# Stack loads split in two halves by heads, the maxima's transfer issued from the scalar engine's queue

## The chip, the cores and the metric

The kernel runs on one core of one Trainium2 chip. The metric is the device time of one execution in microseconds (us), as the median of several runs; lower is better.

## What is computed

For 32 sequences of 256 positions with 128 channels, `x` is normalised to `xn` (layer norm), and the result is `x + attention(xn) + ffn(xn)`:

```python
# attention: 16 heads of 8 channels, causal, rotated q and k, a decay bias per head
scores = einsum('bhqd,bhkd->bhqk', q_rot, k_rot) / sqrt(8) + decay_bias      # 16 heads x 256 x 256
attn = softmax(where(causal, scores, -inf))
out = einsum('bhqk,bhkd->bhqd', attn, v) @ Wo.T
# ffn: routing weights rw over 8 experts, one causal attention with mixed q, k, v, then
# a mixture of 8 experts with gelu, weighted by rw2
q = einsum('btc,ech,bte->bth', n1, q_proj, rw)       # k, v alike; output through o_proj with rw
hs = xn + attn_out
return hs + moe_out
```

## The kernel before

The work of the 32 sequences is a pipeline of 32 steps, `step(n, u, n_x)`, written out by hand once for each engine; each engine has its own program and its own order, and they meet through semaphores. Step n finishes the attentions of sequence n, finds the row maxima of sequence n+1, and computes projections, rotation and routing weights of sequence n+2. After the 32 steps comes the expert part (16 blocks), which the change doesn't touch.

**The stacks.** The scores are computed by matmuls over 128 rows that stand stacked in `qst` and `kst` (bfloat16, 128 partitions x 2 buffers x 16 heads x 256 positions; buffer `u` or `par` is n mod 2). Rows 8 to 55 and the like hold q and k, each split in three bfloat16 parts; other rows hold the decay bias; rows `R_MAX` to `R_MAX + 2` of `qst` hold the negated row maxima, also in three parts. The vector engine leaves the rotated parts in `parts`; SP stores them to DRAM (`store_parts`, semaphore `parts_stored`) and `stacks(b, par, old)` reads them back in stack form: one transfer of zeros to the rows of the maxima, then six into `qst` (8 rows each) and three into `kst` (24, 16 and 8 rows). Ten transfers, all counted by `stack_in`.

**First pass, `unit1`.** Twelve units per sequence (units 0 to 5 read heads 0 to 7, units 6 to 11 heads 8 to 15) compute scores with the maxima's rows at zero; the vector engine takes their row maxima (`row_max`), splits them in parts (`max_parts`), TensorE transposes them (`max_T`), ScalarE copies them to `mT` (`evac_max`), and SP sends `mT` to the maxima's rows of `qst` (`put_max`, semaphore `max_in`).

**Second pass, `unit2`.** Twelve units again, in the same order of heads, now with the maxima subtracted; ScalarE takes the exponential (`exps`). `unit2(n, u, 0)` is the one that waits for `max_in`. In step n the second pass of sequence n stands beside the first pass of sequence n+1.

TensorE's order around a step's start is: ..., `max_T(n+1)`, `att_T(n)`, `oe(n, 0)`, `oe(n, 1)`, `att_out(n)`, `oe(n, 2)` to `oe(n, 7)`, then in the next step `norm_T` (four transposes), `unit2(n+1, ..., 0)`, `qk`, `unit2(..., 1)`, `proj`.

SP's order in a step: store the result of the step before (after `base_done`), load two tiles of `x`, spread the routing weights over all partitions (1 MB, `rep`), `store_parts`, `stacks`, `store_weights`, `put_max`. Stacks of sequence n+2 take the buffer of sequence n, so `stacks` waits until all twelve units of its second pass are done:

```python
sp_.wait_ge(s2_out, UNITS * (b - 1))        # b = n + 2
```

ScalarE ends its step with `evac_max(n+1)` and `evac_att(n)` and begins the next with `evac_norm` (`xnT`, `n1T`, `sqT`).

Lines that the prediction speaks of: L1267 `norm_T`, L1330 and L1337 the first pass's score matmuls, L1360 and L1365 the second pass's, L1308 `weights_T`, L385 the zeros, L391 the stack rows, L396 `store_weights`, L407 `put_max`, L621 `evac_max`, L665 `evac_att`, L589 `evac_norm`, L629 the exponential.

Of the kernel before, what the change touches and what calls it, by code (L numbers as in the profile page):

```python
# [15 lines left out]
S = 256  # L16
D = 128
H = 16
DH = D // H
# [5 lines left out]
UNITS = 3 * NG  # L25
# [15 lines left out]
R_PARTS = 8  # L41
R_MAX = R_PARTS + 6 * DH
Q_SLOTS = ((0, 1, 0), (1, 1, 0), (2, 1, 0), (3, 1, 1), (4, 1, 1), (5, 1, 2))
K_SLOTS = ((0, 3, 0), (3, 2, 0), (5, 1, 0))
KR = P
STACK_DMAS = 1 + len(Q_SLOTS) + len(K_SLOTS)

LN2_LINKS = 3 + 10
# [68 lines left out]
def build(nc, x, w_attn, w_o, log_xi, pi_logit, e_logit, ln1_w, ln1_b, ln2_w, ln2_b, sim1, gates1,  # L117
          q_proj, k_proj, v_proj, o_proj, sim2, gates2, w1, w2, c_ident, c_mask_qk, c_mask_kq, c_pos_freq,
          c_sin_sign, c_pos, c_rank, out):
    scr_parts = nc.dram_tensor("scr_parts", (2, 2, 3, DH, H, S), BF16, kind="Internal").ap()  # L120
# [5 lines left out]
    with ExitStack() as ctx:  # L126
# [3 lines left out]
        def sem(name):  # L130
            return ctx.enter_context(nc.semaphore(name))
# [30 lines left out]
        zeros_b = sb("zeros_b", [3, 1, S], BF16)  # L162
# [98 lines left out]
        rot_chain = sem("rot_chain")  # L261
        parts_out = sem("parts_out")
        parts_stored = sem("parts_stored")
        stack_in = sem("stack_in")
        v_out = sem("v_out")
        v_done = sem("v_done")
        s1_out = sem("s1_out")
# [76 lines left out]
        def _(sp_):  # L344
# [31 lines left out]
                    sp_.dma_start(scr_parts[par, side].rearrange("p d h t -> (d h) p t"),  # L376
                                  parts[:, :, side]).then_inc(parts_stored, 16)

            def stacks(b, par, old):

                if old:

                    sp_.wait_ge(s2_out, UNITS * (b - 1))

                sp_.dma_start(qst[R_MAX:R_MAX + 3, par], zeros_b[:].broadcast_to((3, H, S))).then_inc(stack_in, 16)  # L385
                sp_.wait_ge(parts_stored, 32 * (b + 1))
                for side, dst, slots in ((0, qst, Q_SLOTS), (1, kst, K_SLOTS)):
                    v = scr_parts[par, side].rearrange("p d h t -> (p d) (h t)")
                    for first, n, part in slots:
                        rows = dst[R_PARTS + DH * first:R_PARTS + DH * (first + n), par].rearrange("p h t -> p (h t)")  # L390
                        sp_.dma_start(rows, v[DH * part:DH * (part + n)]).then_inc(stack_in, 16)  # L391

            def store_weights(b, par):

# [3 lines left out]
            def spread_weights(b, par):  # L398
# [2 lines left out]
                sp_.dma_start(rep[:, par].rearrange("p e t -> p (e t)"),  # L401
                              scr_rw[par].rearrange("(o e) t -> o (e t)", o=1).broadcast_to((P, E * S))
                              ).then_inc(rep_in, 16)

            def put_max(b, par):
                sp_.wait_ge(mT_done, b + 1)
                sp_.dma_start(qst[R_MAX:R_MAX + 3, par], mT[:]).then_inc(max_in, 16)  # L407

            def load_x(b, par, dst, arrived):
                src = x_v[b] if isinstance(b, int) else x_v[bass.ds(b, 1)].rearrange("o p i c -> p (o i) c")  # L410
# [6 lines left out]
            def step(n, u, n_x):  # L417


                sp_.wait_ge(base_done, n)  # L420
                if not isinstance(n, int) or n > 0:
                    store_base(n - 1, 1 - u)
                load_x(n, u, xr, xr_in)
                if n_x == 3:

                    sp_.wait_ge(x_in, 16 * (n + 3))
                    load_x(n + 3, 1 - u, xt, x_in)
                if n_x:
                    spread_weights(n + 1, 1 - u)
                if n_x >= 2:  # L430
                    store_parts(n + 2, u)
                if n_x >= 2:
                    stacks(n + 2, u, True)
                    store_weights(n + 2, u)
                if n_x:
                    put_max(n + 1, 1 - u)

            store_parts(0, 0)
            stacks(0, 0, False)
            store_weights(0, 0)  # L440
            spread_weights(0, 0)

# [1 line left out]
            sp_.wait_ge(x_in, 32)  # L444
            load_x(2, 0, xt, x_in)
            store_parts(1, 1)
            stacks(1, 1, False)
            store_weights(1, 1)
            put_max(0, 0)
            step(0, 0, 3)  # L450
            step(1, 1, 3)
            with sp_.Fori(1, NB // 2 - 2) as j:
# [112 lines left out]
        def _(act):  # L565
# [52 lines left out]
            def evac_max(b):  # L618
                act.wait_ge(mT_out, b + 1)
                act.wait_ge(max_in, 16 * b)  # L620
                act.activation(mT[:], ps[0:3 * H, S1[0], 0:S // 2].bitcast(BF16), ACT.Copy).then_inc(mT_done, 1)  # L621

            def exps(n, k, last):

                G, i = divmod(k, 3)
                act.wait_ge(s2_out, UNITS * n + k + 1)
                if i == 0:
                    act.wait_ge(pv_out, NG * n + max(G - 1, 0))
                act.activation(pr[:, G % 2, i], ps[:, S2[k % 2]], ACT.Exp).then_inc(exp_done, 1)  # L629

                if last and k >= UNITS - 2:
                    return
                act.wait_ge(exp_done, UNITS * n + k + 1)
                act.activation(ps[:, S2[k % 2]], seeds[:, 1 if (k + 2) % 3 == 2 else 0], ACT.Copy  # L634
                               ).then_inc(seed_done, 1)
# [27 lines left out]
            def evac_att(n):  # L663
                act.wait_ge(attT_out, n + 1)
                act.activation(attT[:], ps[:, PVB, 0:S], ACT.Copy).then_inc(attT_done, 1)  # L665
# [54 lines left out]
            def step(n, u, n_x):  # L720
                if n_x >= 2:
                    evac_norm(n + 2, u)
                for k in range(3):
                    exps(n, k, n_x == 0)
                if n_x >= 2:
                    evac_logits(n + 2)
                if n_x == 0:
                    evac_norm2(0)
                    square2(0)
                for k in range(3, 8):  # L730
                    exps(n, k, n_x == 0)
                    if n_x == 0 and k == 4:
                        evac_norm2(1)
                        square2(1)
                    if n_x == 0 and k == 5:
                        scale_norm2(2)
                    if k == 6:
                        evac_pv(n, 0)
                    if n_x == 0 and k == 6:
                        evac_logits2(0)  # L740
                    if n_x == 0 and k == 7:
                        scale_norm2(3)
                evac_qk(n)
                exps(n, 8, n_x == 0)
                if n_x >= 2:
                    gate_tanh(n + 2)
                if n_x == 0:
                    evac_norm2(2)
                    square2(2)
                exps(n, 9, n_x == 0)  # L750
                if n_x == 0:
                    gate_tanh2(0)
                soft_exp(n)
                exps(n, 10, n_x == 0)
                exps(n, 11, n_x == 0)
                evac_soft(n)
                if n_x == 0:
                    evac_norm2(3)
                    square2(3)
                evac_pv(n, 1)  # L760
                evac_ve(n)
                if n_x >= 2:
                    evac_weights(n + 2)
                    evac_v(n + 2, u)
                if n_x:
                    evac_max(n + 1)
                evac_att(n)
                if n_x == 1:
                    scale_norm2(0)
                    scale_norm2(1)  # L770
                if n_x == 0:
                    evac_weights2(0)
                    evac_logits2(1)

            for b in range(2):
# [3 lines left out]
                gate_tanh(b)  # L779
                evac_weights(b)  # L780
            evac_max(0)
            step(0, 0, 3)
            step(1, 1, 3)
            with act.Fori(1, NB // 2 - 2) as j:
# [465 lines left out]
        def _(pe):  # L1250
# [60 lines left out]
            def unit1(b, par, k):  # L1311
# [4 lines left out]
                    pe.wait_ge(rwT_done, b + 1 if not isinstance(b, int) or b else 2)  # L1316
                if k == 0:

                    pe.wait_ge(stack_in, 16 * STACK_DMAS * (b + 1 if not isinstance(b, int) or b else 2))
                if k == 0:  # L1320

                    pe.wait_ge(mT_done, b)
# [409 lines left out]
```

## Time and profile before

| what | value |
| --- | --- |
| median of 3 runs | 1439.15 us (1437.37 to 1440.41) |
| time of the profiled execution | 1432.54 us |
| its span | 1430.7 us |
| mean granted TensorE clock | 0.984 of full |
| busy: TensorE matmul, VectorE, ScalarE, GpSimd | 90%, 71%, 53%, 15% |
| DMA, mean | 93 GB/s |

The span is the time from the first to the last instruction of the one execution that the profiler recorded; 1.8 us of its time lie around it. Starts in the rows below are us from the span's start. PE is TensorE, PEld its weight loads, DVE VectorE, ACT ScalarE, POOL GpSimd, SP the engine that only issues transfers; SPq and ACTq are the queues of instructions of SP and ACT, and a transfer's row there shows its issue alone, not its landing. The 32 steps lie between 89 and about 1180 us of the span.

### The profile page before, as it was taken

To read this page: it belongs to the slowest core of one execution; us is meant where nothing else is said; L and a number is where in the kernel's file an instruction comes from. 1 tells how busy PE (TensorE), PEld (TensorE's weight loads), DVE (VectorE), ACT (ScalarE), POOL (GpSimd) and SP (SyncE) were. 2 spreads that over 40 slices of the span, in tenths; PEclk is the share of its full clock that TensorE was granted. 3 is DMA by queue.
4 is the path that set the end of the run, shared out by engine and by line. 5 is a ranking of instruction groups with operands and counts; after the bars stand their busy time and mean duration, and the time that the engine had idled before them with its cause. 6 is when DMAs were issued, how large, how long until landed. Compare 5 with 4: busy or idle time off the path is not lost.

```text
span 1430.7 us, 33751 instructions
## 1 busy us (share of the span) xinstructions
PE 1284.3 (90%) x10686; PEld 1016.5 (71%) x10780; DVE 1021.5 (71%) x3882; ACT 762.4 (53%) x1664; POOL 221.6 (15%) x326
## 2 busy tenths in 40 slices
PE   0369999999999999999999999999999979999999
PEld 0247777777778777777777777777777767777776
DVE  8557777777777777777777777777776656677754
ACT  1125655665555555555555555555555574455532
POOL 4011112111122211111111111112111200000000
PEclk9679999999999999999999999999999999999999
DMA  4423233223333333333222233223223204554344
GB/s 117 94 54 85 76 77 76 75 76 80 79 85 79 78 76 79 83 90 90 77 75 76 75 83 80 76 75 76 75 76 77 58 9 172 204 202 153 149 153 159
DMA packets 89904, 133.33 MB, mean 93 GB/s; under 512 B 9675, under 2 KB 78395, under 8 KB 78523
## 3 DMA queue, kind: packets, MB, share of 16 engines
q1 hardware_dynamic: 89298, 132.10, 32.6%
q14 instruction: 86, 0.70, 0.2%
q8 instruction: 32, 0.52, 0.2%
q10 hardware_dynamic: 488, 0.01, 0.0%
HBM read 108.76 MB, written 21.50 MB: 91 GB/s over the span
## 4 chain that ended last, share of the span: by engine, by line
PE 63%; DVE 15%; DMA 11%; issue 6%; ACT 4%; DVEq 1%; SPq 0%; ACTq 0%
DMA qst<-mT 10%; PE ps L1663 8%; PE ps L1649 8%; PE ps L1401 7%; PE ps L1402 6%; PE ps L1411 6%; PE ps L1275 4%; PE ps L1379 4%; DVE mx L1025 3%; PE ps L1337 3%; PE ps L1360 3%; PE ps L1333 2%; PE ps L1330 2%; PE ps L1436 1%; PE ps L1383 1%
## 5 line engine op out<-in xcount | busy, mean ns | idle before, releaser
L629 ACT ACTIVATE pr<-ps 128x512 f32<-128x512 f32 x384 | 227.7, 593 | 205.4 <-PE ps L1360 166.7
L1025 DVE TENSOR_REDUCE mx<-ps 128x2 f32<-128x512 f32 (+1 forms) x384 | 263.9, 688 | 46.6 <-PE ps L1330 26.2
L634 ACT ACTIVATE ps<-trn 128x512 f32<-128x512 bf16 x382 | 229.8, 601 | 12.1
L530 POOL TENSOR_TENSOR n1s<-rep,n1T 128x256 f32<-128x256 f32 x256 | 177.0, 730 | 277.4 <-DVE mpart L1037 252.9
L1663 PEld LDWEIGHTS ps<-w2s,ats 128*128 128x128 f32 x1024 | 131.7, 192 | 50.4 <-issue 46.5
L1401 PE MATMUL ps<-n1s,wq 128*128 128x256 f32 x512 | 160.6, 396 | 0.0
L1402 PE MATMUL ps<-n1s,wk 128*128 128x256 f32 x512 | 152.8, 380 | 0.0
L1411 PE MATMUL ps<-wv,n1s 128*128 128x128 f32 x1024 | 150.6, 280 | 0.0
L803 ACT ACTIVATE n1s<-ps 128x512 f32<-128x512 f32 x128 | 76.5, 597 | 123.3 <-PE ps L1649 122.1
L1411 PEld LDWEIGHTS ps<-wv,n1s 128*128 128x128 f32 x1024 | 131.9, 192 | 9.0 <-issue 6.3
L1663 PE MATMUL ps<-w2s,ats 128*128 128x128 f32 x1024 | 135.7, 276 | 1.1 <-DVE ats L1207 1.1
L1649 PE MATMUL ps<-rep,w1s 128*128 128x512 f32 x256 | 130.8, 594 | 0.0
L1446 PE MATMUL ps<-wop,ats 128*128 128x128 f32 x1024 | 125.9, 277 | 0.3 <-DVE ats L1074 0.3
L1360 PE MATMUL ps<-qst,kst 128*128 128x256 bf16 x512 | 98.9, 275 | 29.1 <-DMA qst<-mT 29.0
L1446 PEld LDWEIGHTS ps<-wop,ats 128*128 128x128 f32 x1024 | 120.2, 193 | 0.8 <-DVE ats L1074 0.5
L537 POOL TENSOR_TENSOR zt<-xn,rstd 128x256 f32<-128x256 f32 x32 | 19.6, 612 | 646.9 <-DVE rstd L862 646.9
L1402 PEld LDWEIGHTS ps<-n1s,wk 128*128 128x128 f32 x512 | 97.7, 191 | 13.2
L1337 PE MATMUL ps<-kst,qst 128*128 128x256 bf16 x512 | 98.8, 275 | 0.0
L1401 PEld LDWEIGHTS ps<-n1s,wq 128*128 128x128 f32 x512 | 80.0, 192 | 12.3 <-issue 8.6
L1074 DVE TENSOR_TENSOR ats<-rep,ps 128x512 f32<-128x512 f32 (+1 forms) x160 | 81.4, 575 | 10.2 <-PE ps L1437 9.7
L942 DVE TENSOR_TENSOR rott<-ps,cs 128x512 f32<-128x512 f32 x32 | 22.1, 692 | 92.5 <-PE ps L1275 90.0
L589 ACT ACTIVATE xnT<-ps 128x256 f32<-128x256 f32 x32 | 12.3, 383 | 133.4 <-PE ps L1267 128.4
(225 smaller groups left out, 2281.6 us busy)
## 6 DMA issues: line engine op xcount, KB each, us to landing
rep<-scr_rw SPq DMA_DIRECT2D x32, 1024.0 KB, 5.0
qst<-scr_rw SPq DMA_DIRECT2D x16, 1024.0 KB, 6.5
kst<-scr_rw SPq DMA_DIRECT2D x16, 1024.0 KB, 8.3
scr_parts<-parts SPq DMA_DIRECT2D x64, 192.0 KB, 2.3
qst<-scr_parts SPq DMA_DIRECT2D x192, 64.0 KB
kst<-scr_parts SPq DMA_DIRECT2D x32, 192.0 KB
xt<-in_x SPq DMA_DIRECT2D x32, 128.0 KB, 2.3
kst<-scr_parts SPq DMA_DIRECT2D x32, 128.0 KB
```

Of the source, the lines that this page charges most:

```text
L530: pool.tensor_tensor(n1s[:, e], rep[:, par, e], n1T[:, par], ALU.mult).then_inc(n1s_done, 1)
L629: act.activation(pr[:, G % 2, i], ps[:, S2[k % 2]], ACT.Exp).then_inc(exp_done, 1)
L634: act.activation(ps[:, S2[k % 2]], seeds[:, 1 if (k + 2) % 3 == 2 else 0], ACT.Copy).then_inc(seed_done, 1)
L1025: dve.tensor_reduce(mx[:, min(i, 1), h:h + n], ps[:, S1[k % 2]].rearrange("p (h t) -> p h t", h=n), AX_X, ALU.max, negate=True).then_inc(s ...
L1337: ins = mm(bank[:, h * S:(h + 1) * S], qst[0:KR, par, hh, P:S], kst[0:KR, par, hh, :], start=False, stop=True, skip_group_check=True)
L1360: ins = mm(bank[:, h * S:(h + 1) * S], kst[0:KR, u, hh, 0:P], qst[0:KR, u, hh, :], start=False, stop=True, skip_group_check=True)
L1401: mm(ps[:, QKB, 0:S], wq[:, e], n1s[:, e], start=(e == 0), stop=(e == E - 1), skip_group_check=True)
L1402: ins = mm(ps[:, QKB, S:2 * S], wk[:, e], n1s[:, e], start=False, stop=(e == E - 1), skip_group_check=True)
L1411: ins = mm(ps[:, QKB, i * D:(i + 1) * D], n1s[:, e, i * P:(i + 1) * P], wv[:, e], start=(e == 0 and i == 0), stop=(e == E - 1), skip_group ...
L1446: ins = mm(ps[:, G1, i * D:(i + 1) * D], ats[:, e, i * P:(i + 1) * P], wop[:, e], start=(e == 0 and i == 0), stop=(e == E - 1), skip_group ...
L1649: mm(ps[:, UP[k % 4]], w1s[:, e], n2T[t % 8], start=True, stop=True).then_inc(up_out, 1)
L1663: ins = mm(ps[:, MOE[t % 2], i * D:(i + 1) * D], hgs[:, k % 2, i * P:(i + 1) * P], w2s[:, e], start=(e == 0 and i == 0), stop=(e == E - 1) ...
```

## The change

`stacks` gets a fourth argument, the half. Each half loads the rows of eight heads, with its own zeros and its own semaphore of a pair. The first half waits only for the first six units of the second pass that reads its buffer, the second half for all twelve. Per sequence SP issues 20 transfers of half the size in place of 10. `unit1` waits for the first half ahead of unit 0 and for the second ahead of unit 6. `put_max` goes from SP's program to ScalarE's, where it stands behind `evac_att`.

```diff
+HALF_HEADS = H // 2
...
-        stack_in = sem("stack_in")
+        stack_in = [sem("stack_lo_in"), sem("stack_hi_in")]
...
-            def stacks(b, par, old):
-
+            def stacks(b, par, old, half):
+
+                hh = slice(HALF_HEADS * half, HALF_HEADS * (half + 1))
                 if old:
 
-                    sp_.wait_ge(s2_out, UNITS * (b - 1))
-
-                sp_.dma_start(qst[R_MAX:R_MAX + 3, par], zeros_b[:].broadcast_to((3, H, S))).then_inc(stack_in, 16)
+                    sp_.wait_ge(s2_out, UNITS * (b - 2) + UNITS // 2 * (half + 1))
+
+                sp_.dma_start(qst[R_MAX:R_MAX + 3, par, hh], zeros_b[:].broadcast_to((3, HALF_HEADS, S))
+                              ).then_inc(stack_in[half], 16)
                 sp_.wait_ge(parts_stored, 32 * (b + 1))
                 for side, dst, slots in ((0, qst, Q_SLOTS), (1, kst, K_SLOTS)):
-                    v = scr_parts[par, side].rearrange("p d h t -> (p d) (h t)")
+                    v = scr_parts[par, side].rearrange("p d h t -> (p d) h t")
                     for first, n, part in slots:
-                        rows = dst[R_PARTS + DH * first:R_PARTS + DH * (first + n), par].rearrange("p h t -> p (h t)")
-                        sp_.dma_start(rows, v[DH * part:DH * (part + n)]).then_inc(stack_in, 16)
+                        rows = dst[R_PARTS + DH * first:R_PARTS + DH * (first + n), par, hh]
+                        sp_.dma_start(rows, v[DH * part:DH * (part + n), hh]).then_inc(stack_in[half], 16)
...
-            def put_max(b, par):
-                sp_.wait_ge(mT_done, b + 1)
-                sp_.dma_start(qst[R_MAX:R_MAX + 3, par], mT[:]).then_inc(max_in, 16)
...
                 if n_x >= 2:
-                    stacks(n + 2, u, True)
+                    stacks(n + 2, u, True, 0)
+                    stacks(n + 2, u, True, 1)
                     store_weights(n + 2, u)
-                if n_x:
-                    put_max(n + 1, 1 - u)
...
+            def put_max(b, par):
+                act.wait_ge(mT_done, b + 1)
+                act.dma_start(qst[R_MAX:R_MAX + 3, par], mT[:]).then_inc(max_in, 16)
...
                 evac_att(n)
+                if n_x:
+                    put_max(n + 1, 1 - u)
...
                 if k == 0:
 
-                    pe.wait_ge(stack_in, 16 * STACK_DMAS * (b + 1 if not isinstance(b, int) or b else 2))
+                    pe.wait_ge(stack_in[0], 16 * STACK_DMAS * (b + 1 if not isinstance(b, int) or b else 2))
+                if k == UNITS // 2:
+
+                    pe.wait_ge(stack_in[1], 16 * STACK_DMAS * (b + 1 if not isinstance(b, int) or b else 2))
```

SP's program in a steady step, before (in square brackets the semaphores it waits for):

```order
L376 DMA scr_parts<-parts 128x3x256 [waits parts_out]
L376 DMA scr_parts<-parts 128x3x256
L385 DMA qst<-zeros_b 3x16x256 [waits s2_out]
L391 DMA qst<-scr_parts 8x4096 [waits parts_stored]
L391 DMA qst<-scr_parts 8x4096 x5
L391 DMA kst<-scr_parts 24x4096
L391 DMA kst<-scr_parts 16x4096
L391 DMA kst<-scr_parts 8x4096
L396 DMA scr_rw<-rwT 16x128 [waits rwT_done]
L407 DMA qst<-mT 3x16x256 [waits mT_done]
L415 DMA scr_base<-bs 128x256 [waits base_done]
```

The same place in the changed kernel, from the first half's zeros on:

```order
L387 DMA qst<-zeros_b 3x8x256 [waits s2_out]
L394 DMA qst<-scr_parts 8x2048 [waits parts_stored]
L394 DMA qst<-scr_parts 8x2048 x5
L394 DMA kst<-scr_parts 24x2048
L394 DMA kst<-scr_parts 16x2048
L394 DMA kst<-scr_parts 8x2048
L387 DMA qst<-zeros_b 3x8x256 [waits s2_out]
L394 DMA qst<-scr_parts 8x2048 [waits parts_stored]
...
L399 DMA scr_rw<-rwT 16x128 [waits rwT_done]
L414 DMA scr_base<-bs 128x256 [waits base_done]
```

The ten transfers have become two groups of ten with half as many columns, each group behind its own wait for the second pass, and the maxima's transfer is gone from SP.

ScalarE's program at the end of a step, before:

```order
L616 ACTIVATE rwT<-ps 16x128 [waits rw_stored,rwT_out]
L602 ACTIVATE vst<-ps 128x4x4x8 [waits v_out]
L602 ACTIVATE vst<-ps 128x4x4x8
L621 ACTIVATE mT<-ps 48x256 [waits max_in,mT_out]
L665 ACTIVATE attT<-ps 128x256 [waits attT_out]
```

and in the changed kernel:

```order
L615 ACTIVATE rwT<-ps 16x128 [waits rw_stored,rwT_out]
L601 ACTIVATE vst<-ps 128x4x4x8 [waits v_out]
L601 ACTIVATE vst<-ps 128x4x4x8
L620 ACTIVATE mT<-ps 48x256 [waits max_in,mT_out]
L668 ACTIVATE attT<-ps 128x256 [waits attT_out]
L624 DMA qst<-mT 3x16x256 [waits mT_done]
```

The maxima's transfer now stands on ScalarE, one instruction behind the copy that it waits for. TensorE's order of matmuls is the same in both.

## Rows read from the trace of the kernel before

**Rows 1.** The page: busy time of TensorE; shares of the chain by line

```profile
PE 1284.3 (90%) x10686; PEld 1016.5 (71%) x10780; DVE 1021.5 (71%) x3882; ACT 762.4 (53%) x1664; POOL 221.6 (15%) x326
...
DMA qst<-mT 10%; PE ps L1663 8%; PE ps L1649 8%; PE ps L1401 7%; PE ps L1402 6%; PE ps L1411 6%; PE ps L1275 4%; PE ps L1379 4%; DVE mx L1025 3%; PE ps L1337 3%; PE ps L1360 3%; PE ps L1333 2%; PE ps L1330 2%; PE ps L1436 1%; PE ps L1383 1%
```

**Rows 2.** Who waited for whom: us in total, times, longest us

```profile
PE ps L1360 <- DMA qst<-mT: 29.0, 29, 3.0
...
PEld ps L1360 <- DMA qst<-mT: 7.9, 5, 3.2
```

**Rows 3.** Timeline, TensorE, one step's sixth unit, the next's start: start, us, [idle before]

```profile
615.59 0.39 PE L1365 MATMUL ps<-qst,kst 128*128 128x128 bf16 x4
...
638.10 0.38 PE L1267 MATMUL ps<-ident,zt 128*128 128x128 f32 x2
639.54 0.39 PE L1360 MATMUL ps<-qst,kst 128*128 128x256 bf16 x2 [1.06 <-DMA qst<-mT]
```

**Rows 4.** Timeline, SP's queue, one step: start, us of the issue

```profile
616.77 0.91 SPq L376 DMA_DIRECT2D scr_parts<-parts  x2
627.69 0.78 SPq L385 DMA_DIRECT2D qst<-zeros_b  x1
628.59 2.25 SPq L391 DMA_DIRECT2D qst<-scr_parts  x6
630.88 1.04 SPq L391 DMA_DIRECT2D kst<-scr_parts  x3
...
634.36 0.76 SPq L407 DMA_DIRECT2D qst<-mT  x1
```

**Rows 5.** Stretches of that step: us, PE, PEld, DVE, ACT, POOL, PEclk, DMA share, GB/s

```profile
628.00:633.00 5.00, 4.65 (x48) 3.85 (x47) 4.36 (x23) 2.48 (x6) 0.67 (x1) 1.00 0.52 95
633.00:638.00 5.00, 5.00 (x48) 4.97 (x47) 2.88 (x6) 1.23 (x5) 4.87 (x8) 1.00 0.50 72
```

**Rows 6.** Timeline, TensorE: starts of second passes in steps 1, 10, 11, 29, 30

```profile
127.99 0.39 PE L1360 MATMUL ps<-qst,kst 128*128 128x256 bf16 x2 [0.55 <-DMA qst<-mT]
...
433.29 0.38 PE L1267 MATMUL ps<-ident,zt 128*128 128x128 f32 x2
433.51 0.38 PE L1360 MATMUL ps<-qst,kst 128*128 128x256 bf16 x2
...
466.35 0.38 PE L1267 MATMUL ps<-ident,zt 128*128 128x128 f32 x2
...
1083.95 0.39 PE L1360 MATMUL ps<-qst,kst 128*128 128x256 bf16 x2 [1.13 <-DMA qst<-mT]
...
1117.24 0.39 PE L1360 MATMUL ps<-qst,kst 128*128 128x256 bf16 x2 [0.98 <-DMA qst<-mT]
```

**Rows 7.** Timeline, ScalarE, the same step's end and the next one's start

```profile
633.96 0.37 ACT L621 ACTIVATE mT<-ps 48x256 bf16<-48x256 bf16 x1
634.23 0.37 ACT L665 ACTIVATE attT<-ps 128x256 f32<-128x256 f32 x1
638.60 0.38 ACT L589 ACTIVATE xnT<-ps 128x256 f32<-128x256 f32 x1 [4.00 <-PE ps L1267]
...
640.05 0.60 ACT L629 ACTIVATE pr<-ps 128x512 f32<-128x512 f32 x1 [0.17 <-PE ps L1360]
```

**Rows 8.** Timeline, SP and TensorE at the first maxima's transfer (no stack loads beside it)

```profile
89.44 0.75 SPq L407 DMA_DIRECT2D qst<-mT  x1
...
92.40 0.61 PE L1360 MATMUL ps<-qst,kst 128*128 128x256 bf16 x2 [2.95 <-DMA qst<-mT]
```

**Rows 9.** Timeline, ScalarE, the program's start: first and last of its five transfers, their first reader

```profile
0.75 1.24 ACTq L569 DMA_DIRECT2D pig<-in_pi_logit  x1
...
7.02 0.20 ACT L576 ACTIVATE pig<-pig 128x1 f32<-128x1 f32 x1 [1.88 <-DMA sg<-in_gates]
```

**Rows 10.** Timeline, before the steps: last stack loads, TensorE's routing transpose, first unit

```profile
70.12 1.41 SPq L391 DMA_DIRECT2D kst<-scr_parts  x3
...
75.58 0.38 PE L1308 MATMUL ps<-ident,gt 128*16 128x128 f32 x1 [15.35 <-DVE gt L1006]
78.33 0.63 PE L1330 MATMUL ps<-kst,qst 128*128 128x128 bf16 x4 [2.37 <-DMA kst<-scr_parts]
```

More of the change, by code:

```diff
@@ L432, in step @@
                 if n_x >= 2:
-                    stacks(n + 2, u, True)
+                    stacks(n + 2, u, True, 0)
+                    stacks(n + 2, u, True, 1)
                     store_weights(n + 2, u)
-                if n_x:
-                    put_max(n + 1, 1 - u)
             store_parts(0, 0)
-            stacks(0, 0, False)
+            stacks(0, 0, False, 0)
+            stacks(0, 0, False, 1)
             store_weights(0, 0)
@@ L446, in _ @@
             store_parts(1, 1)
-            stacks(1, 1, False)
+            stacks(1, 1, False, 0)
+            stacks(1, 1, False, 1)
             store_weights(1, 1)
-            put_max(0, 0)
             step(0, 0, 3)
@@ L781, in _ @@
             evac_max(0)
+            put_max(0, 0)
             step(0, 0, 3)
```

## The prediction

> **What bounds the kernel now.** The page first: matmuls keep TensorE busy 90% of the span, and in the chain that ended last one transfer stands above every line of TensorE, `qst<-mT`, with 10% [rows 1]. A share of the chain counts from issue to landing and says nothing of how much of it TensorE would have spent working anyway, so the table of waits is next: TensorE stood idle for this transfer 29 times, 29.0 us in all, and in a few steps the wait is booked on its weight loads, 7.9 us in 5 [rows 2]. Nearly every one of the 32 steps is there. The timeline of one step shows the place: the last transpose of `norm_T` starts at 638.10 and the first matmul of the second pass at 639.54, after 1.06 us of idling [rows 3].
>
> Why is it late? SP issues it at 634.36, the moment `mT` is copied (633.96 + 0.37) [rows 4, 7]. TensorE gets it 5.2 us later. Where the same transfer runs with no stack loads ahead of it, at the first maxima, 2.96 us pass (89.44 to 92.40) [rows 8]. So some 2.2 us are queueing: SP had issued the ten stack transfers from 627.69 to 631.92 [rows 4], 792 KB by their shapes, the zeros among them, and the DMA engines moved 95 GB/s until 633 and 72 GB/s until 638 [rows 5], that is 475 and 360 KB: the loads take until about 638, and the maxima come behind them in the same queue.
>
> What TensorE would do without the wait is also in the trace. At 433.51 one step begins 0.22 us behind the last transpose, with no idling at all; the next step's last transpose starts at 466.35, so that an undelayed start there would be at 466.57: **33.06 us** for a step [rows 6]. The 28 steps from 127.99 to 1083.95 take 955.96 us, 34.14 each [rows 6]. The undelayed step isn't longer in its body, so the other engines kept up with it.
>
> **The change part by part.**
>
> *First half early.* The sixth unit of this pass starts at 615.59 [rows 3], so its wait is already met when `store_parts` goes out at 616.77 [rows 4]; the first ten small transfers can go out between 617.5 and 623, while SP before only waited there for the pass's end. What is queued behind this on SP is the second half, which may not start before 627.69 anyway, and then `store_weights`. Cost on the path: nothing.
>
> *Second half.* It starts at 627.69 as before, with ten issues again. Zeros and rows have half the bytes; I leave the issue time at the old 4.1 us [rows 4], so the last is out at 631.9. It moves 396 KB. In the kernel before, 475 KB had been moved by 633 [rows 5], so the second half should be landed by about 633 to 634, before the maxima are issued. This is bounded by the other end, that a transfer's time doesn't shrink with its size: then the loads last until 638 as now. I take the first, since the rate in these rows is what many transfers at once give; the other end is rival A. The Trainium skill speaks for that other end: its page "DMA: Bandwidth & Descriptors", section "Rules for kernel authors", says to coalesce, and that under 64 KB one pays mostly overhead; the `qst` pieces go from 64 to 32 KB. By it the sum would be rival A's. No row here shows a transfer of 32 KB beside one of 64 KB.
>
> *Maxima on ScalarE's queue.* It stands behind `evac_att`, which ends at 634.23 + 0.37 = 634.60 [rows 7], so it is issued 0.24 us later than now, and holds ScalarE for the 0.76 us of an issue [rows 4]. Who waits behind it: `evac_norm`, which now starts at 638.60 after 4.00 us of idling [rows 7]; it is covered, and if that idle time were gone it would cost at most 0.76 us a step. With the undisturbed 2.96 us the maxima land at 637.6. TensorE can start unit 0 at 638.10 + 0.22 = 638.32. **Margin 0.7 us.** The landing from ScalarE's queue is bounded from below by these 2.96, and from above by the only transfers the trace shows there, the five at the start: issued from 0.75 on, read at 7.02, 6.27 us for all [rows 9]. I take 2.96: same bytes, same shape, and the rows 9 hold five issues and a cold start.
>
> *What moves on TensorE.* Every start of a second pass in steps 1 to 30 comes at the undelayed time. 28 steps x (34.14 - 33.06) = 30.2 us, plus the waits of steps 1 and 30, which are not in them, 0.55 and 0.98 [rows 6]: **31.8 us**. Lower bound: the idle time in the table less step 0's, 29.0 - 2.95 = 26 us [rows 2, 8]. Step 0's wait of 2.95 stays, since nothing was ahead of it; step 31 has none. Late next in a step is nothing new: ScalarE's `xnT` is released by the transposes, which don't move against the step, and its first exponential starts at 640.05, held until then by its own copies (idle before it only 0.17) [rows 7]. It can't come earlier by the 1.2 us that TensorE does, which would matter if the unit after next had to wait for it; the step at 433.51 had just this start and lost nothing [rows 6].
>
> *Prologue.* TensorE waits 2.37 us for the last stack rows, issued by 71.5, before its first unit at 78.33, though the routing transpose was done by 76.0 [rows 10]. Now unit 0 needs only the first half of both sequences, issued first. Gain between 0 and 2.37; against it, ten more issues for each of two sequences, 4.1 us each, ahead of `store_weights`. That they delay the routing weights by 1 us is possible, so the bounds are +1 and -2.4. I take -2.
>
> **Sum:** 31.8 + 2 = 33.8 us, say 34. The profiled execution took 1432.54 (span 1430.7, 1.84 around it), so it would take 1398.5. It was 6.6 us faster than the median of the runs; on the median, 1439.15 - 34 = **1405 us**.
>
> **Rivals.**
>
> A. *The pieces cost by their number.* The halves then take as long as the whole, the DMA engines are still full at 636, and the maxima, though in a queue of their own, share the engines with them. For: the rate fell from 95 to 72 GB/s in the second stretch without more transfers being issued [rows 5], so something other than bytes counts. Against: rows of 4 KB are still long. Half of the 31.8 us remains lost: 1439.15 - 16 - 1 = 1422 us. A rule of the Trainium skill (same page, "Issuing engines are not separate DMA queues") goes the same way: transfers from different engines run on the same 16 DMA engines and interleave, so the new queue alone brings little while loads are in flight.
>
> B. *ScalarE's queue lands late (slower).* If a transfer issued there takes the 6.27 us of rows 9, it lands at 634.60 + 6.27 = 640.87, against 639.54 now: 1.33 x 30 = 40 us lost, 2 won in the prologue: 1477 us. The point from which it decides is a landing time of 4.9 us. Against: these were five issues (one of 1.24 us) with small pieces to 128 partitions [rows 9].
>
> C. *The wait only changes its name.* The start comes earlier, but ScalarE's exponentials or VectorE's maxima don't, and TensorE loses it again inside the step. For: ScalarE's first exponential can't move [rows 7]. Against: the undelayed step of 33.06 us [rows 6]. Time: only the prologue won, 1437 us, within what can be told from no change.
>
> **How the numbers follow.** The forecast (maxima hidden) 0.79; A 0.10; B 0.05; C 0.06. A difference of 0.2% (2.9 us) is about what a measurement of this kernel can tell from no change. Faster: forecast and A, 0.89. Same: C, 0.06. Slower: B, 0.05. The forecast's own range is 1397 (all of 2.4 in the prologue, 5 us of scatter between executions) to 1412 (26 us of waits, nothing in the prologue). I extend it to A's 1422 so that with part of the forecast's misses 8 in 10 are surely held: 1397 to 1422.
>
> **What would show it.** Right: TensorE's wait for `qst<-mT` down from 29.0 us to about 3 (step 0); steps of 33.1 us; the transfer issued by ScalarE about 0.3 us behind `attT`'s start plus 0.37; DMA activity at 617 to 623 where there was none, and less of it after 634. Wrong, by A: waits of 0.3 to 0.8 us remain ahead of L1360 and the DMA engines stay busy until 637. By B: waits above 1.3 us at the same place. By C: no wait for the maxima, but new idle time of TensorE behind ScalarE's `ps<-trn` or VectorE's `mx`, and steps still at 34 us. The number that would refute the sum is a step time over 33.5 us.

## The result, and the profile after

| | before | changed |
| --- | --- | --- |
| median | 1438.26 us (4 runs, 1435.13 to 1440.41) | 1393.86 us (4 runs, 1393.15 to 1394.32) |
| ratio | | 0.971, 95% interval 0.9687 to 0.9732 |
| time of the profiled execution | 1432.54 us | 1394.32 us |
| its span | 1430.7 us | 1392.5 us |
| mean granted TensorE clock | 0.984 | 0.985 |

The changed kernel is faster by 44 us where 34 had been forecast. Its time, 1393.9, lies below the range of 1397 to 1422.

The page of the changed kernel, parts 1 and 4, against [rows 1]:

```profile
PE 1280.9 (92%) x10780; PEld 1017.3 (73%) x10780; DVE 1020.6 (73%) x3882; ACT 760.8 (55%) x1664; POOL 221.6 (16%) x326
...
PE 72%; DVE 16%; issue 5%; ACT 2%; SPq 1%; DMA 1%; DVEq 1%; ACTq 0%
```

The engines do the same work in a shorter span, and DMA is down to 1% of the chain. The table of waits, against [rows 2]:

```profile
PEld ps L1369 <- DMA qst<-mT: 3.2, 1, 3.2
...
PE ps L1369 <- DMA qst<-mT: 2.9, 1, 2.9
```

One wait is left of 29, that of step 0. A step's start on TensorE in the changed kernel (start us, us, what):

```profile
617.91 0.38 PE L1273 MATMUL ps<-ident,zt 128*128 128x128 f32 x2
618.12 0.38 PE L1369 MATMUL ps<-qst,kst 128*128 128x256 bf16 x2
618.34 0.60 PE L1410 MATMUL ps<-n1s,wq 128*128 128x256 f32 x2
618.78 0.59 PE L1411 MATMUL ps<-n1s,wk 128*128 128x256 f32 x2
619.21 0.38 PE L1369 MATMUL ps<-qst,kst 128*128 128x256 bf16 x2
```

The second pass begins 0.21 us behind the last transpose where it was 1.44 us [rows 3]; in all of steps 1 to 29 it is 0.21 or 0.22. The rows that follow the wait in the kernel before:

```profile
639.86 0.69 PE L1401 MATMUL ps<-n1s,wq 128*128 128x256 f32 x2
640.39 0.59 PE L1402 MATMUL ps<-n1s,wk 128*128 128x256 f32 x2
640.82 0.38 PE L1360 MATMUL ps<-qst,kst 128*128 128x256 bf16 x2
```

From the first unit to the second it took 1.28 us there (639.54 to 640.82) and takes 1.09 us now (618.12 to 619.21), with the same matmuls between. So a late start cost more than its idle time here, but not everywhere. The weight load between the two, in this step and in step 28, which also starts late (1.31 us):

```profile
639.85 0.30 PEld L1401 LDWEIGHTS ps<-n1s,wq 128*128 128x128 f32 x2 [0.20 <-issue]
...
1050.19 0.30 PEld L1401 LDWEIGHTS ps<-n1s,wq 128*128 128x128 f32 x2
```

Steps 2 to 27 stand in a loop in every engine's program; the others are written out. In the loop a late start is followed by 1.16 or 1.28 us, and the weight load idles with no releaser; in steps 1, 28 and 29 it is followed by 1.09 or 1.10 us, as behind no wait. What is paid are therefore instructions of TensorE's own program that the loop has between the wait and that load and that are otherwise over by then. That they compute the loop's semaphore counts is likely and was not tried.

The first and the last regular start of the steps, changed kernel:

```profile
123.33 0.38 PE L1369 MATMUL ps<-qst,kst 128*128 128x256 bf16 x2
...
1046.86 0.38 PE L1369 MATMUL ps<-qst,kst 128*128 128x256 bf16 x2
```

28 steps take 923.53 us, 32.98 each, against 34.14 [rows 6]. The steps of the loop take 33.06 and 32.97 us in turn, and the two written-out ones among the 28 take 32.58 each.

SP's and ScalarE's queues in one step of the changed kernel, against [rows 4, 7]:

```profile
597.60 0.78 SPq L387 DMA_DIRECT2D qst<-zeros_b  x1
599.33 2.20 SPq L394 DMA_DIRECT2D qst<-scr_parts  x6
601.57 1.05 SPq L394 DMA_DIRECT2D kst<-scr_parts  x3
607.50 0.77 SPq L387 DMA_DIRECT2D qst<-zeros_b  x1
608.32 2.13 SPq L394 DMA_DIRECT2D qst<-scr_parts  x6
610.48 1.04 SPq L394 DMA_DIRECT2D kst<-scr_parts  x3
```

```profile
614.03 0.37 ACT L668 ACTIVATE attT<-ps 128x256 f32<-128x256 f32 x1
614.17 0.72 ACTq L624 DMA_DIRECT2D qst<-mT  x1
```

Both halves go out where they were expected, and the maxima's issue needn't wait for `attT`'s copy to end: it overlaps it. Last, two stretches of the changed kernel in which the halves move, and then the ten busy microseconds of the kernel before (columns as in [rows 5]: the last two are the DMA engines' mean busy share and GB/s):

```profile
600.00:604.00 4.00, 3.66 (x33) 2.86 (x35) 3.90 (x24) 3.08 (x7) 0.00 (x0) 1.00 0.33 98
609.00:613.00 4.00, 3.65 (x38) 3.00 (x38) 3.24 (x17) 1.32 (x4) 0.86 (x2) 1.00 0.36 101
```

```profile
629.00:634.00 5.00, 4.65 (x49) 3.87 (x48) 4.25 (x21) 2.15 (x8) 1.67 (x3) 1.00 0.66 108
634.00:639.00 5.00, 4.48 (x40) 4.23 (x38) 2.79 (x7) 1.00 (x5) 3.87 (x6) 1.00 0.38 62
```

Divide the rate by the share and by 16, the number of DMA engines that the share is a mean of, and there is the rate of one busy engine: 98 / (0.33 x 16) = 18.6 and 101 / (0.36 x 16) = 17.5 GB/s now, 10.2 in both stretches before. The halves don't only come in two parts; each byte also costs less engine time. No step of the prediction had that, and the experiments are mostly about it.

**Where the 38.2 us between the two spans are.** Start of the first second pass: 92.40 [rows 8] to 88.47, 3.9 us. Step 0: 35.59 to 34.86, 0.7 us. The 28 steps: 955.96 to 923.53, 32.4 us, of which the delays behind the last transpose are 29.0 and the slower start after a wait, paid in the loop's 26 steps, 3.4 (a step without its delay took 33.11 us on average and takes 32.98). From step 29's start to the end: 346.75 to 345.64, 1.1 us.

### The profile page after: what moved, and what is told of

The parts are those of the page before. It is cut to its first block, busy times and chain, and to the rows that moved or that the text cites. A ratio compares the mean times of both kernels' runs of the same rounds, so it can differ in the third digit from the quotient of the medians.

```text
span 1392.5 us, 34210 instructions
## 1 busy us (share of the span) xinstructions
PE 1280.9 (92%) x10780; PEld 1017.3 (73%) x10780; DVE 1020.6 (73%) x3882; ACT 760.8 (55%) x1664; POOL 221.6 (16%) x326
## 4 chain that ended last, share of the span: by engine, by line
PE 72%; DVE 16%; issue 5%; ACT 2%; SPq 1%; DMA 1%; DVEq 1%; ACTq 0%
PE ps L1672 8%; PE ps L1455 8%; PE ps L1658 8%; PE ps L1410 7%; PE ps L1411 6%; PE ps L1420 6%; PE ps L1281 4%; PE ps L1388 4%; DVE mx L1031 3%; PE ps L1346 3%; PE ps L1369 2%; PE ps L1342 2%; PE ps L1445 1%; PE ps L1392 1%; PE ps L1374 1%
## 5 line engine op out<-in xcount | busy, mean ns | idle before, releaser
L1342 PE MATMUL ps<-mask_qk,identb 128*128 128x256 bf16 x256 | 71.3, 279 | 12.7 <-DVE mx L1031 12.1
```

## The experiments

Three explanations of the gain (theories, below) stood at first. **E**: the maxima land in time because half of the loads has gone early. **Q**: because they have a queue of their own. **P**: because rows of 4 KB are faster on the DMA engines than rows of 8 KB. A fourth came up later, **R**: because fewer bytes are issued per microsecond. "Before" ran beside each group; its median was 1437.42 us over the 19 runs of the first group (early_sp, late_act, whole_act, before_again), 1435.95 over the 11 of the second (whole_paced_act, probe_late_act, prologue_whole, x_first) and 1436.54 over the 9 of the third (the rest).

**early_sp: the maxima back on SP.**

```diff
+            def put_max(b, par):
+                sp_.wait_ge(mT_done, b + 1)
+                sp_.dma_start(qst[R_MAX:R_MAX + 3, par], mT[:]).then_inc(max_in, 16)
...
                     store_weights(n + 2, u)
+                if n_x:
+                    put_max(n + 1, 1 - u)
...
                 evac_att(n)
-                if n_x:
-                    put_max(n + 1, 1 - u)
```

> The changed kernel with the maxima's transfer back on SP, in its old place behind store_weights; halves as in the change. Theory E (half the loads gone early, the rest over before the maxima are issued): the queue doesn't matter, the maxima land about 3.0 us after their issue, TensorE's wait for them is about 3 us in all (step 0 alone), time 1394 us within 3. Theory Q (the maxima need a queue of their own): waits of 0.3 us or more a step remain, 1404 us or more.

Measured: 1394.04 us (4 runs, 1392.79 to 1395.28), as the changed kernel; one wait of 2.9 us; no start delayed in steps 1 to 29. The trace also holds the time of each transfer's last completion event. From the maxima's issue to that event, steps 1 to 29, it is 2.67 to 2.78 us here from SP's queue and 2.63 to 2.80 in the changed kernel from ScalarE's, the median 2.69 in both. With early halves ScalarE's queue gives nothing.

**whole_act: the kernel before with only the queue changed.**

```diff
                     store_weights(n + 2, u)
-                if n_x:
-                    put_max(n + 1, 1 - u)
...
+            def put_max(b, par):
+                act.wait_ge(mT_done, b + 1)
+                act.dma_start(qst[R_MAX:R_MAX + 3, par], mT[:]).then_inc(max_in, 16)
...
                 evac_att(n)
+                if n_x:
+                    put_max(n + 1, 1 - u)
```

> The kernel before with one edit: the maxima's transfer on ScalarE's queue behind the copy of att; stacks whole. Theory Q (they stood behind the loads in one queue, and no more): the waits go, the prologue's 4 us stay, 1398 to 1402 us. Theory P or E (the DMA engines themselves are full until 638): the maxima still land late, waits of 0.5 to 1.5 us a step, 1420 to 1438 us.

Measured: 1438.68 us (10 runs, 1433.82 to 1441.88), ratio 1.0012 (0.9992 to 1.0031): no change. Its waits, its maxima's issue and the start that waits for them:

```profile
PE ps L1360 <- DMA qst<-mT: 30.0, 28, 2.8
```

```profile
635.57 0.72 ACTq L618 DMA_DIRECT2D qst<-mT  x1
```

```profile
640.28 0.39 PE L1360 MATMUL ps<-qst,kst 128*128 128x256 bf16 x2 [0.60 <-DMA qst<-mT]
```

Alone in their queue the maxima need 4.7 us in this step, against 2.96 undisturbed [rows 8]. That is no gain on the 5.2 of [rows 4]: the times differ from step to step, and by the completion events the median of steps 1 to 29 is 5.0 us here (3.6 to 5.6) and 5.0 in the kernel before (3.5 to 5.6). Theory Q falls.

**late_act: halves, but neither of them early.**

```diff
-                    sp_.wait_ge(s2_out, UNITS * (b - 2) + UNITS // 2 * (half + 1))
+                    sp_.wait_ge(s2_out, UNITS * (b - 1))
```

> The changed kernel, but both halves wait for all twelve units, so nothing is loaded early; the maxima stay on ScalarE's queue. All 20 transfers are issued from the pass's end on, some 8 us, and are in flight when the maxima go out. Theory P (rows of 8 KB are slow on the DMA engines, rows of 4 KB aren't, and a queue of its own lets the maxima pass): waits of less than 0.3 us a step, 1394 to 1402 us. Theory E (only what is loaded early counts): the maxima share the engines with the loads, waits of about 1 us a step remain, 1420 to 1435 us.

Measured: 1395.30 us (4 runs, 1394.14 to 1396.41), one wait of 2.8 us, two starts late by 0.15 and 0.25 us. So nearly all of the gain comes without going early, and E falls as the only cause. The loads' ten microseconds in late_act:

```profile
609.00:614.00 5.00, 4.65 (x48) 3.85 (x47) 4.35 (x22) 2.47 (x6) 0.68 (x1) 1.00 0.29 81
614.00:619.00 5.00, 5.00 (x48) 4.97 (x47) 2.88 (x6) 1.23 (x5) 4.86 (x8) 1.00 0.34 89
```

A busy engine moves 17.5 and 16.4 GB/s, though all 792 KB go out in one go, over 8.9 us in place of 4.2. Whole stacks differ from that in two things, the size of a row and the rate of issue; the next two runs part them.

**whole_paced_act: rows of 8 KB, issued slowly.**

```diff
+ZERO_HEADS = (2, 2, 2, 2, 2, 1, 1, 1, 1, 1, 1)
...
                         sp_.dma_start(rows, v[DH * part:DH * (part + n)]).then_inc(stack_in, 16)
+                        zeros()
```

`zeros()` sends the zeros of the next one or two heads.

> The kernel with whole stacks and the maxima on ScalarE's queue, but the zeros cut in eleven pieces that stand between the nine loads of rows, so that SP issues 20 transfers as in late_act, over 6 to 8 us, with the same bytes and rows of 8 KB. Theory P (a row of 8 KB in one piece is what costs): the waits stay as in whole_act, 0.5 us or more a step, 1425 to 1442 us. Theory R (the slower rate of issue is what helped late_act): waits below 0.3 us a step, 1396 to 1405 us.

Measured: 1422.53 us (4 runs, 1421.43 to 1424.29), ratio 0.9908 (0.9873 to 0.9943). The time is in the range of neither theory, and its rows say why. A stretch of its loads, and its waits:

```profile
632.00:637.00 5.00, 5.00 (x46) 4.96 (x45) 2.82 (x7) 1.00 (x5) 4.21 (x7) 1.00 0.32 83
```

```profile
PE ps L1338 <- DMA qst<-zeros_b: 17.3, 29, 5.4
...
PE ps L1372 <- DMA qst<-mT: 3.3, 2, 2.9
```

All but one short wait for the maxima, beside that of step 0, are gone as R has it, with rows of 8 KB, and a busy engine moves 83 / (0.32 x 16) = 16.2 GB/s. The maxima are issued at 632.70, in the midst of the loads (626.03 to 638.87), and by the completion events they land 2.96 to 3.21 us after their issue in steps 1 to 29. In their place stands a wait of my own making: the stacks are complete later than the first pass wants them (29 waits, 17.3 us), since issuing takes 12.8 us, not the 6 to 8 expected, so until the next step, and nothing is split by heads. The prologue is also slower (first second pass at 98.4, not 92.4). So small rows aren't needed to remove the maxima's wait.

**halves_two_queues: rows of 4 KB, issued fast.**

```diff
                 exps(n, 11, n_x == 0)
+                if n_x >= 2:
+                    stacks_hi(n + 2, u)
```

`stacks_hi` is the second half's ten issues in ScalarE's program; both halves wait for all twelve units, as in late_act.

> late_act, but in the steps the second half is issued by ScalarE behind its last exponential while SP issues the first, so that 768 KB in rows of 4 KB go out in some 4 us, as fast as the whole stacks in the kernel before. ScalarE's program is held for those 3 to 4 us, so the time says little (above 1394 us, perhaps 1500); the DMA rate in the 5 us behind the pass's end is what is read. Theory R (too many bytes issued at once slow the DMA engines, whatever the rows' size): the rate per busy engine falls to 10 to 12 GB/s as in the kernel before (95 GB/s at a share of 0.52). Theory P (only rows of 8 KB are slow): it stays at 16 to 18 GB/s as in late_act (89 GB/s at 0.34).

Measured: one run, 1480.2 us; ScalarE is held for some 4.1 us a step by its ten issues. Its loads:

```profile
616.00:620.00 4.00, 2.60 (x31) 1.92 (x29) 2.88 (x15) 0.35 (x2) 0.66 (x1) 1.00 0.46 122
620.00:624.00 4.00, 3.26 (x26) 3.02 (x27) 2.50 (x8) 2.20 (x8) 4.00 (x7) 1.00 0.55 83
```

A busy engine starts at 122 / (0.46 x 16) = 16.6 GB/s and falls to 83 / (0.55 x 16) = 9.4 once the two streams have piled up; over both stretches it is 12.7, between the 10.2 of whole stacks and the 16 to 18 of slow issue. So rows of 4 KB slow down too when many bytes are issued at once. The rest of the way isn't told apart. The packets of the stack rows alone, over 29 or 30 loads of the steps in each run (the changed kernel's halves counted singly), with the KB issued per us and the rate of a busy engine:

| run | rows | KB issued per us | GB/s, median (range) |
| --- | --- | --- | --- |
| before | 8 KB | 231 | 10.7 (10.0 to 13.1) |
| halves_two_queues | 4 KB | 177 | 12.9 (12.1 to 14.7) |
| changed | 4 KB | 120 | 18.4 (16.3 to 22.2) |
| late_act | 4 KB | 101 | 17.3 (16.0 to 18.5) |
| whole_paced_act | 8 KB | 73 | 17.8 (16.5 to 20.7) |

Slow issue alone restores the rate with either row. But halves_two_queues wasn't quite as fast as whole stacks, 177 against 231 KB per us, and a sequence's rows took 3.8 us of an engine's time in it, against 4.6 before and 2.85 in late_act: nearly half of the saving is still there. Whether that half is the somewhat slower issue, the shorter rows (P) or the second queue, no run here tells.

**probe_late_act and probe_after: when the maxima land.** Both put one wait on TensorE, the first into late_act, the second into the changed kernel:

```diff
                 att_out(n)
+                if n_x:
+                    pe.wait_ge(max_in, 16 * (n + 2))
```

> late_act with a wait for the maxima put on TensorE right behind att_out, so that it stands still until they land and the landing can be read. Theory P: with rows of 4 KB still in flight they land 2.9 to 3.5 us after the issue, against 4.6 us in whole_act. Rival: they land at 3.7 us or more and late_act hides them only just. The wait itself makes each step 1 to 3 us longer.

> The changed kernel with a wait for the maxima on TensorE right behind att_out, to read when they land. Theory E (nothing in flight any more): 2.9 to 3.1 us after the issue in every step, which leaves 1 us of margin to the second pass's start; in probe_late_act, with loads in flight, it was 3.4 to 3.9 us. Rival: 3.4 us or more here too. Each step 1.5 to 2.5 us longer by the wait.

Issue and end of the wait, first in probe_late_act, then in probe_after:

```profile
637.89 0.72 ACTq L624 DMA_DIRECT2D qst<-mT  x1
```

```profile
641.68 4.57 PE L1455 MATMUL ps<-wop,ats 128*128 128x128 f32 x24 [2.79 <-DMA qst<-mT]
```

```profile
656.40 0.72 ACTq L624 DMA_DIRECT2D qst<-mT  x1
...
659.28 1.14 PE L1455 MATMUL ps<-wop,ats 128*128 128x128 f32 x5 [1.88 <-DMA qst<-mT]
```

With late halves it takes 3.8 us here, and 3.4 and 3.9 in the two other steps I read; with the early half gone, 2.9 us (2.8 in another). By the completion events, which come 0.1 to 0.2 us ahead of the matmul, the maxima land after 2.8 to 4.0 us in probe_late_act (median 3.4) and 2.7 to 2.8 in probe_after; without a probe it is 2.7 to 4.1 (median 3.55) in late_act and 2.6 to 2.8 in the changed kernel. From the issue to the time at which the second pass wants them there are 3.95 us in both kernels (614.17 to 618.12). This is what the early start buys: a margin of 1.1 us in every step, where late halves have 0.3 us in the median and none in two steps, and most of the 1.4 us between the medians of late_act and the changed kernel (their profiled spans differ by 1.5, of which the 28 steps are 1.0). Neither side of the first expectation held in every step: Theory P's 2.9 to 3.5 us holds in about half of them, the rival's 3.7 or more in others. TensorE's standing still made both slower (1521.9 and 1481.6 us), as meant.

**prologue_whole: the change without its prologue.**

```diff
-            stacks(0, 0, False, 0)
-            stacks(0, 0, False, 1)
+            whole_stacks(0, 0)
...
-            stacks(1, 1, False, 0)
-            stacks(1, 1, False, 1)
+            whole_stacks(1, 1)
```

> The changed kernel, but the stacks of sequences 0 and 1, ahead of the steps, are loaded in whole transfers as before. If the prologue gave 3.9 us of the change and the steps the rest: 1397 to 1399 us, the first second pass 3 to 5 us later than in the changed kernel. Rival (the prologue's gain is scatter between executions): within 1 us of the changed kernel.

Measured: 1399.23 us (4 runs, 1398.35 to 1400.63), 5.4 us over the changed kernel, a little more than expected. In the profiled pair the spans differ by 5.7 us: 4.8 of it stand in the prologue (first second pass at 93.24, not 88.47), and 1.1 behind step 29's start, which the edit doesn't touch. Its prologue, then the same places in the changed kernel:

```profile
75.67 0.38 PE L1321 MATMUL ps<-ident,gt 128*16 128x128 f32 x1 [15.26 <-DVE gt L1019]
78.98 0.59 PE L1342 MATMUL ps<-mask_qk,identb 128*128 128x512 bf16 x1 [2.92 <-DMA kst<-scr_parts]
```

```profile
73.82 0.38 PE L1314 MATMUL ps<-ident,gt 128*16 128x128 f32 x1 [13.87 <-DVE gt L1012]
74.03 0.59 PE L1335 MATMUL ps<-mask_qk,identb 128*128 128x512 bf16 x1
```

Two things come together: the wait for the stacks is gone, and the routing transpose itself is 1.85 us earlier, because the loads of sequence 0 are over sooner and with them the transfers queued behind them. Among these the load of `x` for sequence 2, issued at 60.46, lands at 65.17, where it lands at 67.02 in prologue_whole: 1.85 us here too. That VectorE's chain hangs on it is what the next run tries.

**x_first: that load ahead of the stacks.**

```diff
+            sp_.wait_ge(ln_out, 1)
+            sp_.wait_ge(x_in, 32)
+            load_x(2, 0, xt, x_in)
             store_parts(0, 0)
             stacks(0, 0, False, 0)
...
             spread_weights(0, 0)
-            sp_.wait_ge(ln_out, 1)
-            sp_.wait_ge(x_in, 32)
-            load_x(2, 0, xt, x_in)
```

> The changed kernel with the load of x for sequence 2 issued ahead of the first stacks' loads rather than behind them and the spreading of the weights. VectorE waits 2.2 us for it in the changed kernel and the routing chain hangs on it. If that wait is on the path: 1391 to 1393 us. Rival (the chain is held by sequence 1's stored parts instead): no change, 1394 us.

Measured: 1391.71 us (6 runs, 1391.25 to 1392.42), ratio 0.9691 (0.9665 to 0.9716). The runs of the two kernels don't overlap, and the profile shows the cause: the transpose and the first second pass come earlier.

```profile
71.63 0.38 PE L1314 MATMUL ps<-ident,gt 128*16 128x128 f32 x1 [11.11 <-DVE gt L1012]
72.26 0.59 PE L1335 MATMUL ps<-mask_qk,identb 128*128 128x512 bf16 x1 [0.25 <-DMA kst<-scr_parts]
...
86.70 0.60 PE L1369 MATMUL ps<-qst,kst 128*128 128x256 bf16 x2 [2.90 <-DMA qst<-mT]
```

It is the fastest version of these, 2.1 us below the changed kernel, though that was measured in another group of runs.

**x_first_late_rep: the spreading moved too.**

```diff
-            spread_weights(0, 0)
...
             stacks(1, 1, False, 0)
+            spread_weights(0, 0)
             stacks(1, 1, False, 1)
```

> x_first, and the first spreading of the routing weights (1 MB, needed only after the first maxima) goes behind the first half of sequence 1's stacks, so that it no longer stands ahead of sequence 1's stored parts. If those parts' landing is on the path in the prologue: 0.5 to 1.5 us less than x_first, 1390 to 1391 us. Rival (VectorE's routing chain is the path): 1391.7 us as x_first.

Measured: 1394.74 us (5 runs, 1393.37 to 1395.02), a miss: 3 us slower than x_first, which was measured in another group of runs; the profiled spans differ by 2.6. TensorE reached the seventh unit and stood:

```profile
77.97 0.61 PE L1335 MATMUL ps<-mask_qk,identb 128*128 128x512 bf16 x1 [1.27 <-DMA kst<-scr_parts]
```

The 1 MB now stood ahead of the second half of the stacks, which is wanted 6 us after the first. The parts' landing came only 0.5 us earlier (65.79, not 66.29); moving a large transfer out of one wait put it into the next. That is the smaller part of the loss: the seventh unit starts 0.6 us later than in x_first, and the first second pass 1.8 (88.52, not 86.70). Between them the granted TensorE clock differs. In x_first it stood at 1.00 (2.4 GHz) from 77.7 to 84.5, after TensorE had worked from 72.26 with no stop over 0.25 us; here it stayed at 0.50 (1.2 GHz) until 94.3, and the way from the seventh unit to the maxima's transposes took 6.78 us in place of 5.70. That the clock stayed down because of the stop is a guess which no run tried.

**before_again: the kernel before, unchanged.**

> The kernel before, unchanged, to profile a second execution of it and to see its scatter. Theory: its executions differ by how late the maxima land, so that the sum over the steps of the delay behind the last transpose differs between the two profiled executions by as much as their spans do (within 2 us), while a step without its delay stays at 33.1 to 33.2 us. Rival: the scatter is elsewhere (steps' bodies, expert part), and the sums of delays agree within 1 us though the spans differ by several. Time 1438 us within 4, spread over 3 us.

Measured: 1437.90 us (10 runs, 1433.29 to 1441.16). Its profiled execution has a span of 1435.2 us, 4.5 over that of the first. The delays behind the last transpose, summed over steps 1 to 29, are 33.7 us against 29.7, 3.9 more before rounding, and the steps' bodies are the same within 0.01 us (33.11). The rest, 0.2 us from the prologue and step 0 and 0.4 elsewhere, is small. So these two executions of the kernel before differ mostly by how late the maxima land.

## Why the prediction was right, and where it was wrong

**Right: the place, the direction, the new waits.** The wait ahead of L1360 fell from 29 to one, that of step 0, with 2.9 us. No other engine took its place, so rival C (given 0.06) didn't come; the argument from the one undelayed step, 33.06 us, held in all 28, none of which takes over 33.07. ScalarE's queue isn't late, so rival B fell: 2.9 us to land against its 6.27. The margin was put at 0.7 us and is 1.1.

**Wrong: the size, in three terms.** 1405 was 11 us too high.

1. *"It was 6.6 us faster than the median of the runs; on the median, 1439.15 - 34 = 1405 us."* This step failed most. It carries the gap between the profiled execution and the median over into the changed kernel, 7.1 us with the changed kernel's own difference of 0.5. The gap was made mostly of the thing that goes: in before_again the execution with more delay is longer by nearly the same amount, and of the kernels without the wait none scatters over more than 3 us (4 to 6 runs each), while those with it scatter over 8 (before_again and whole_act, 10 runs each). Against the profiled execution alone the forecast was 1398.5, and it is 1394.3. The range inherits the step, and its lower end doesn't even follow from its own terms: 31.8 and 2.4 us off 1439.15, and 5 more for scatter, give 1400, not 1397; 26 off give 1413, not 1412.
2. *"28 steps x (34.14 - 33.06)"*, with the ends 31.8 us: it is 34.3 (0.7 + 32.4 + 1.1). The undelayed step of 33.06 was the longest of three kinds. In the loop they take 33.06 and 32.97 in turn, and 33.26 and 33.05 when they start late; the two written-out steps take 32.58. The average is 32.98, and 28 x 0.08 are the 2.2 us that the steps gave above the term. The other 0.3 are the two ends, 1.8 for 1.5.
3. *"Gain between 0 and 2.37 ... I take -2"* for the prologue: it is 3.9 us in the profiled pair, and 4.8 between the profiled executions of the changed kernel and prologue_whole. The bound took the one wait that the halves remove and missed that the loads of sequence 0 would be over sooner and let everything queued behind them through.

**Wrong in its reason: the queue.** The prediction had "the maxima come behind them in the same queue" as the cause of the lateness, "some 2.2 us are queueing". whole_act gives them a queue of their own and gains nothing. The rule of the Trainium skill cited under rival A, that transfers from different engines share the same 16 DMA engines and interleave ("DMA: Bandwidth & Descriptors", section "Issuing engines are not separate DMA queues"), agrees with this: with loads in flight the median landing is 5.0 us from either queue, and there is no gain in time. The same page of the Trainium skill advises to coalesce (section "Rules for kernel authors"), which the prediction named for the end at which halves take as long as the whole. Here twice as many pieces of half the size took less engine time, not as much or more. But size isn't what made it: pieces of 64 KB and more, issued slowly, moved 16.2 GB/s per busy engine, and pieces of 32 KB and more, issued fast, fell to 9.4.

**Right in part by luck: "the second half should be landed by about 633 to 634".** I reckoned with the old rate. The second half is issued from 607.50 to 611.5, and from 613 to 617 the DMA engines are busy for 4% of the time: it is over within 5.5 us, in time, but at a rate per busy engine that no row of the kernel before had shown. late_act shows that even all the bytes in one go, in halves, would have done.

## What to carry to other kernels

When a small transfer is late behind large ones, look at how many bytes are put under way at once before giving it another queue: issued half as fast (late_act), the same loads here took 40% less engine time, and the small one landed in time from ScalarE's queue; with half of the loads gone earlier, it landed in time from either queue. When a wait with a varying length goes, the gap between the profiled execution and the median can go with it, so subtract from the profiled execution. A wait can cost more than the idle time in its row, as it did in the loop's steps here; compare the instructions behind it with the same ones behind no wait. And one undelayed step isn't every step: look for the kinds that a loop and the steps written out around it make.

## What the runs showed of the hardware

- The rate of a busy DMA engine fell as more bytes were issued at once: 16 to 18.6 GB/s with up to some 400 KB in 4 us, with rows of 4 KB and of 8 KB alike, 10.2 GB/s with 792 KB in 4.2 us and rows of 8 KB, 9.4 GB/s at the worst with rows of 4 KB. How much of this the rows' length has a share in, and what gets in whose way (the engines used by transfers of 8 rows, the memory, the writes), no run here tells; it stays open.
- After a wait inside the loop, TensorE's next unit came 0.07 to 0.19 us later than behind no wait (1.16 and 1.28 us against 1.09 for the same matmuls); in steps written out it came no later (1.09 and 1.10). In the step shown the weight load idled 0.20 us with no releaser.
- Out of ScalarE's queue and out of SP's, the 24 KB of the maxima landed in the same time: 2.69 us in the median with no loads in flight, 5.0 with whole stacks in flight.
- A transfer issued from ScalarE begins while the copy ahead of it still runs: `attT` from 614.03 for 0.37 us, the issue at 614.17. It held ScalarE 0.72 us, within 4.00 us of idling.
- Not tried: late halves with the maxima on SP, where SP's own issuing, some 8 us, would stand ahead of them.
